# Late value tiles spread over 21 units of the score pass, and table and weight copies moved off ScalarE

## The chip, the cores and the metric

The kernel runs on one NeuronCore of a Trainium2 chip. Its engines work side by side and are ordered by semaphores alone: TensorE (PE in the profile; PEld is its weight load), VectorE (DVE), ScalarE (ACT), GpSimd (POOL), and SyncE (SP), which issues most transfers. The metric is the device time of one execution in microseconds; where several runs are shown, their median.

## The reference

One transformer block on x of 4 x 1024 tokens with 256 features, in float32. Cut to what matters:

```python
x = x + _layernorm(attention(_layernorm(x)))          # 16 heads of 16 dims, rotary positions
    q, k, v = x @ Wq.T + bq, x @ Wk.T + bk, x @ Wv.T + bv     # q and k then rotated
    attn = softmax(q @ k.T / 4); out = (attn @ v) @ Wo.T + bo
x = x + _layernorm(moe(_layernorm(x)))                # 8 experts of hidden size 684
    dist = sqrt(squared distance of each token to 8 centroids)
    w, sel = top_k(dist, 2); w = softmax(w)           # the two farthest centroids
    out = sum over the two: w * ((silu(x @ Wg + bg) * (x @ W1 + b1)) @ W2 + b2)
```

## The kernel before, in words

**Start.** The 4096 tokens are cut into 8 blocks (NB) of 512. For each, VectorE takes the statistics (`stats`, L881 and L884), ScalarE the standard deviation (`deviation`, L1274), VectorE its inverse and the offset (`invert`, L888 and L890), and ScalarE writes the normalised rows (`normalise`, L1281). TensorE turns them (`turn_x`, L1482), ScalarE copies them out of PSUM (`save_xt`, L1287), and TensorE projects q and k (`project`, L1493), which VectorE rotates (`rope_unit`, L912 to L921) with GpSimd (L724, L729) and ScalarE (`high`, L1301). Three things must be ready once: the cosine and sine tables, turned by TensorE into four PSUM banks (L1469) and copied to SBUF (L1316); the q and k weights and biases in rotation order (L1307, L1311); and the biases as columns, by four small matmuls into bank 6 (L1474), copied by L1318. ScalarE does all eleven of these copies, between `deviation(0)` and `normalise(0)`.

**Value tiles.** `project_v(m, half)` (L1509) projects 256 tokens to the values of all heads: four matmuls of 128x256 (eight records in the trace), saved by ScalarE (`save_v`, L1294), stored by SP (`store_v`, L465). The first four tiles (EARLY_V = 2 blocks) are made within the start; the other twelve are late.

**Score pass.** The scores are made twice. The first pass finds the row maxima: `max_scores` (L1528) writes, for unit m and pair a, two matmuls of 48x512 into two banks, and VectorE reduces the pair with one instruction (`reduce_max`, L942). There are two pairs of banks (4 and 5, 6 and 7), and

```python
if half == 0:
    after(pe, s_max, 2 * (UNITS * g + m) + a - 1)
```

lets TensorE refill a pair only when the reduce of the unit before has read it. A group (four heads of one batch element) has UNITS = 16 units. The main loop makes the scores of group g again, with exponentials and weighted sums (L1540, L1346, L1554), and in the same units the first pass of what lies LEAD = 5 units ahead of the next group. So before the main loop stand 16 units of group 0 and 5 of group 1: 21 units. The twelve late value tiles stand there too, one behind each of units 0 to 11. TensorE waits for all late tiles to be saved before the main loop. The maxima, split and turned (L753, L755, L948), go through DRAM into the stacks (`load_max_rows`, L492 and L497), once for each half of a group.

Every engine has its own instruction list, in the order in which the code of its block is written: nothing is reordered by a scheduler.

## Time and profile before

| | us |
|---|---|
| median of three runs | 1600.58 (1593.86 to 1622.9) |
| the profiled execution, whole | 1592.43 |
| its span, first to last instruction | 1590.5 |
| mean granted TensorE clock over the span | 0.949 |

The span falls into the start (to about 98 us), the first score pass (to 155), the main loop over 16 groups (to about 800), the output projection with norms and routing (to about 955) and the experts. All times below are from the span's start. The granted clock is a share of 2.4 GHz: 1.00 is the upper of its two levels, 0.50 the lower (1.2 GHz).

### The profile page before, as it was taken

The page shows a single profiled execution, that of the slowest core. Times are in us where ns is not written, and L with a number is a line of the kernel's source. Part 1 is how long each engine was busy: PE and PEld are TensorE (multiplying, and loading weights), DVE is VectorE, ACT ScalarE, POOL GpSimd, SP SyncE. Part 2 cuts the span into 40 slices and gives each one's busy share as a digit, 9 for nine tenths or more (in the row PEclk, how much of TensorE's full clock was granted, in tenths as well). Part 3 has the DMA queues.
Part 4 walks back from the last instruction along what each step waited for, and adds up shares of the span by engine and source line. Part 5 has one row for each costly group of instructions (what it writes and reads, how often), then busy time and mean ns, then how long its engine had stood idle before and what let it go on. Part 6 is the DMA issues. An engine that isn't in the chain of part 4 may idle for free.

```text
span 1590.5 us, 29998 instructions
## 1 busy us (share of the span) xinstructions
PE 1446.7 (91%) x9435; PEld 800.9 (50%) x9436; DVE 1107.6 (70%) x1978; ACT 852.3 (54%) x1624; POOL 427.4 (27%) x411
## 2 busy tenths in 40 slices
PE   7989999999999999999999438999999999999950
PEld 4444333333333333333355226777777777777740
DVE  5989899999999989999026774555555555455525
ACT  5531788888888878888865321222222222222215
POOL 3760000000000010001014143444444444444425
PEclk9997899999999999999999759999999999999985
DMA  5887146334545554550429623222212222121136
GB/s 171 241 254 129 44 98 169 65 71 81 88 82 89 100 88 64 82 89 16 158 54 213 225 98 91 33 33 33 31 32 33 33 33 33 33 33 31 32 85 199
DMA packets 125116, 141.80 MB, mean 89 GB/s; under 512 B 55131, under 2 KB 98949, under 8 KB 125030
## 3 DMA queue, kind: packets, MB, share of 16 engines
q1 hardware_dynamic: 109126, 121.98, 33.2%
q0 software_dynamic: 15904, 18.66, 7.2%
q8 instruction: 56, 0.92, 0.2%
q14 instruction: 30, 0.25, 0.1%
HBM read 86.30 MB, written 54.30 MB: 88 GB/s over the span
## 4 chain that ended last, share of the span: by engine, by line
PE 78%; DVE 7%; issue 5%; ACT 4%; DMA 2%; SPq 2%; POOL 1%; DVEq 0%; POOLq 0%; ACTq 0%
PE psum L1681 20%; PE psum L1528 18%; PE psum L1554 16%; PE psum L1700 11%; PE psum L1691 3%; PE psum L1509 2%; PE psum L1540 2%; PE psum L1612 1%; PE psum L1493 1%; ACT work L1346 1%; DVE mx L942 1%; ACT weights L1356 1%; PE psum L1667 1%; PE psum L1610 1%; DVE work L1141 1%
## 5 line engine op out<-in xcount | busy, mean ns | idle before, releaser
L942 DVE TENSOR_REDUCE mx<-psum 128x1 f32<-128x1024 f32 x512 | 622.9, 1222 | 29.2 <-PE psum L1528 26.3
L1346 ACT ACTIVATE work<-psum 128x512 f32<-128x512 f32 x1024 | 556.7, 597 | 106.1 <-PE psum L1540 43.8
L1528 PE MATMUL psum<-stack 48*128 48x512 f32 x1024 | 379.3, 457 | 6.7 <-DVE mx L942 6.0
L1540 PE MATMUL psum<-stack 50*128 50x512 f32 x1024 | 379.1, 450 | 0.0
L1681 PE MATMUL psum<-weights,values 128*128 x1136 | 341.1, 454 | 0.6 <-DVE values L1161 0.6
L1554 PE MATMUL psum<-work,values 128*32 128x256 f32 x4096 | 330.5, 395 | 9.2 <-ACT weights L1356 9.2
L1528 PEld LDWEIGHTS psum<-stack 48*128 48x128 f32 x1024 | 154.2, 191 | 221.7 <-DVE mx L942 184.7
L1681 PEld LDWEIGHTS psum<-weights,values 128*128 128x128 f32 x1136 | 211.8, 192 | 99.2 <-issue 3.1
L1423 ACT ACTIVATE values<-values 128x342 f32<-128x342 f32 x142 | 69.3, 488 | 250.1 <-DVE values L1173 250.1
L1700 PE MATMUL psum<-weights,work 114*128 (+1 forms) x852 | 198.7, 383 | 1.3 <-ACT work L1434 0.8
L1554 PEld LDWEIGHTS psum<-work,values 128*32 128x32 f32 x4096 | 82.5, 108 | 198.2 <-ACT work L1346 100.5
L1700 PEld LDWEIGHTS psum<-weights,work 114*128 114x128 f32 (+1 forms) x852 | 158.0, 192 | 21.3 <-issue 1.8
L1540 PEld LDWEIGHTS psum<-stack 50*128 50x128 f32 x1024 | 153.8, 188 | 17.3 <-ACT work L1346 17.3
L829 POOL DMA_INDIRECT values<-xn_d,at_x x71 | 70.0, 986 | 280.9 <-DVE at_w L1204 275.5
L1429 ACT ACTIVATE work<-psum,dots 128x256 f32<-128x256 f32 x71 | 33.6, 473 | 201.3 <-PE psum L1700 196.7
L1173 DVE TENSOR_TENSOR values<-psum,work 128x342 f32<-128x342 f32 x142 | 73.1, 515 | 92.0 <-PE psum L1681 68.1
L836 POOL DMA_INDIRECT y_d<-work,at_y x71 | 115.2, 1622 | 39.7 <-issue 27.2
L1176 DVE TENSOR_TENSOR values<-psum,work 128x342 f32<-128x342 f32 x142 | 73.1, 515 | 62.2 <-PE psum L1681 62.2
L1192 DVE COPY work<-psum 114x256 f32<-114x256 f32 x71 | 30.2, 425 | 118.2 <-PE psum L1691 118.2
L753 POOL CAST m<-mx 128x16 fp32r<-128x16 f32 x32 | 6.3, 197 | 376.4 <-DVE mx L942 376.4
L1181 DVE TENSOR_TENSOR values<-values 128x342 f32<-128x342 f32 x142 | 73.3, 516 | 14.7
L744 POOL TENSOR_TENSOR values<-weights,dots 128x512 f32<-128x512 f32 x16 | 20.5, 1283 | 225.4 <-issue 225.2
(184 smaller groups left out, 1190.6 us busy)
## 6 DMA issues: line engine op xcount, KB each, us to landing
stack<-qk_scr SPq DMA_DIRECT2D x192, 128.0 KB, 6.1
qk_scr<-weights SPq DMA_DIRECT2D x16, 1024.0 KB, 4.8
weights<-in_w SPq DMA_DIRECT2D x8, 1368.0 KB, 7.1
ot_scr<-weights SPq DMA_DIRECT2D x16, 512.0 KB, 3.2
weights<-in_w SPq DMA_DIRECT2D x8, 684.0 KB
work<-in_b SPq DMA_DIRECT2D x8, 684.0 KB, 8.8
y_d<-zeros SPq DMA_DIRECT2D x1, 4224.0 KB, 14.3
v_scr<-weights SPq DMA_DIRECT2D x32, 128.0 KB, 2.5
```

The costliest lines, as they stand in the source:

```text
L829: pool.indirect_dma_start(out=x_row, out_offset=None, in_=xn2_d, in_offset=bass.IndirectOffsetOnAxis(ap=at_x[:, 0:1], axis=0)).then_inc(s_ ...
L836: pool.indirect_dma_start(out=y_d, out_offset=bass.IndirectOffsetOnAxis(ap=at_y[:, 0:1], axis=0), in_=y_row, in_offset=None, compute_op=AL ...
L942: dve.tensor_reduce(mx[:, r, a, t:t + 1], bank(4 + 2 * a, 2), AX, ALU.max, negate=True).then_inc(s_max, 1)
L1173: dve.tensor_tensor(gates[c], bank(2 * c)[:, 0:CH], bias(0), ALU.add).then_inc(s_gb, 1)
L1176: dve.tensor_tensor(hid[:, CH * c:CH * (c + 1)], bank(2 * c + 1)[:, 0:CH], bias(HID), ALU.add).then_inc(s_ub, 1)
L1181: dve.tensor_tensor(hid[:, CH * c:CH * (c + 1)], hid[:, CH * c:CH * (c + 1)], gates[c], ALU.mult).then_inc(s_hid, 1)
L1346: act.activation(pt[u % 4][:, j, :], bank((c + HG * u + n) % 3), ACT.Exp, scale=SC).then_inc(s_exp, 1)
L1528: ins = pe.matmul(bank(4 + 2 * a + half), qs[t3][at:at + QROWS, r, P * t:P * (t + 1)], ks[t3][at:at + QROWS, r, 512 * half:512 * (half + 1 ...
L1540: pe.matmul(bank((t3 + HG * u + n) % 3), ks[t3][at:at + MROWS, r, P * st:P * (st + 1)], qs[t3][at:at + MROWS, r, 512 * half:512 * (half + ...
L1554: last = pe.matmul(bank(3)[32 * j:32 * (j + 1), at:at + 256], vg[p][:, st, j, :], pt[u % 4][:, j, at:at + 256], start=st + part == 0, stop ...
L1681: last = pe.matmul(dst, x_t[:, k, :], w1_sb[:, bass.ds(e, 1), k, col:col + CH].rearrange("p a n -> p (a n)"), start=k == 0, stop=k == KC - 1)
L1700: last = pe.matmul(bank(7)[:, 0:C], h_t[0:rows, k, :], w2_sb[0:rows, bass.ds(e, 1), k, :].rearrange("p a n -> p (a n)"), start=k == 0, sto ...
```

## The change

Three edits. The eleven copies leave ScalarE: GpSimd reorders the weights and the bias row (six copies), VectorE copies the four tables and the bias columns, right behind `invert(0)`; TensorE makes the bias columns behind `turn_x(0)` instead of ahead of it. The twelve late value tiles are spread over all 21 units by an integer rule: behind units 1, 3, 5, 6, 8, 10, 12, 13, 15, 17, 19 and 20. And SP sends the two maxima loads of group 0 behind the stores of blocks 3 and 5 instead of 5 and 7.

```diff
@@ -584,9 +584,8 @@
             load_stacks(sp, 0, 1)
             for m in range(EARLY_V, NB):
                 store_v(sp, m)
-                if m == 5:
-                    load_max_rows(sp, 0, 0, 0)
-            load_max_rows(sp, 0, 0, 1)
+                if m in (3, 5):
+                    load_max_rows(sp, 0, 0, (m - 3) // 2)
             sp.wait_ge(s_ones, 3)
             load_stacks(sp, 0, 2)
             for parts_of in s_pst:
@@ -714,6 +713,15 @@
                 pool.wait_ge(s_pad, n + 1)
             pool.memset(cent_t[:, :, :], 0.0).then_inc(s_pad, 1)
 
+            pool.wait_ge(s_wqkv, 32)
+            for k in range(KC):
+                for i in range(2):
+                    pool.tensor_copy(w_turn[:, k, i, :, :].rearrange("p s (d h) -> p s d h", h=H),
+                                     w_qkv[:, k, C * i:C * (i + 1)].rearrange("p (h s d) -> p s d h", s=2, d=HALF)).then_inc(s_wp, 1)
+            for i in range(2):
+                pool.tensor_copy(b_turn[0:1, i, :, :].rearrange("p s (d h) -> p s d h", h=H),
+                                 b_row[0:1, C * i:C * (i + 1)].rearrange("p (h s d) -> p s d h", s=2, d=HALF)).then_inc(s_wp, 1)
+
             def rotate(w):
 
                 p = w % 2
@@ -923,6 +931,11 @@
             stats(0)
             spread_tables()
             invert(0)
+            for n, (table, at) in enumerate(((cos_t, 0), (cos_t, 512), (sin_t, 0), (sin_t, 512))):
+                dve.wait_ge(s_tab, n + 1)
+                dve.tensor_copy(table[:, at:at + 512], bank(n)).then_inc(s_tabs, 1)
+            dve.wait_ge(s_bt, 1)
+            dve.tensor_copy(b_c[:, :], bank(6)[:, 0:4]).then_inc(s_bc, 1)
             stats(1)
             invert(1)
             for m in range(NB):
@@ -1301,21 +1314,6 @@
                 act.activation(hl[w % 4][:, 0, :, :].bitcast(F32R), rr[w % 2], ACT.Copy).then_inc(s_hi, 1)
 
             deviation(0)
-            act.wait_ge(s_wqkv, 32)
-            for k in range(KC):
-                for i in range(2):
-                    act.activation(w_turn[:, k, i, :, :].rearrange("p s (d h) -> p s d h", h=H),
-                                   w_qkv[:, k, C * i:C * (i + 1)].rearrange("p (h s d) -> p s d h", s=2, d=HALF),
-                                   ACT.Copy).then_inc(s_wp, 1)
-            for i in range(2):
-                act.activation(b_turn[0:1, i, :, :].rearrange("p s (d h) -> p s d h", h=H),
-                               b_row[0:1, C * i:C * (i + 1)].rearrange("p (h s d) -> p s d h", s=2, d=HALF),
-                               ACT.Copy).then_inc(s_wp, 1)
-            for n, (table, at) in enumerate(((cos_t, 0), (cos_t, 512), (sin_t, 0), (sin_t, 512))):
-                act.wait_ge(s_tab, n + 1)
-                act.activation(table[:, at:at + 512], bank(n), ACT.Copy).then_inc(s_tabs, 1)
-            act.wait_ge(s_bt, 1)
-            act.activation(b_c[:, :], bank(6)[:, 0:4], ACT.Copy).then_inc(s_bc, 1)
             normalise(0)
             save_xt(0)
             deviation(1)
@@ -1468,12 +1466,6 @@
                     src = spread[n // 2][:, 4 * (n % 2) + a, :, :].rearrange("p d h -> p (d h)")
                     last = pe.transpose(bank(n)[:, P * a:P * (a + 1)], src, ident[:, :])
                 last.then_inc(s_tab, 1)
-            pe.wait_ge(s_wp, 6)
-            for i in range(2):
-                for s in range(2):
-                    last = pe.matmul(bank(6)[:, 2 * i + s:2 * i + s + 1], b_turn[0:1, i, s, :], ones_f[0:1, 0:1], start=True, stop=True)
-            last.then_inc(s_bt, 1)
-
             def turn_x(m):
                 pe.wait_ge(s_xn, TB * (m + 1))
                 for k in range(KC):
@@ -1511,6 +1503,12 @@
                 last.then_inc(s_vp, 1)
 
             turn_x(0)
+            pe.wait_ge(s_wp, 6)
+            for i in range(2):
+                for s in range(2):
+                    last = pe.matmul(bank(6)[:, 2 * i + s:2 * i + s + 1], b_turn[0:1, i, s, :], ones_f[0:1, 0:1], start=True, stop=True)
+            last.then_inc(s_bt, 1)
+
             for m in range(NB):
                 project(2 * m)
                 if m + 1 < NB:
@@ -1582,12 +1580,13 @@
                 for m in range([UNITS, LEAD][g]):
                     for n in range(HG):
                         max_scores(g, g, m, n // 2, n % 2)
-                    b = 2 * EARLY_V + m
-                    if g == 0 and b < 2 * NB:
-                        if m == 0:
-                            pe.wait_ge(s_r1, NU)
-                            pe.wait_ge(s_x1, NU)
-                        project_v(b // 2, b % 2)
+                    unit = UNITS * g + m
+                    late = 2 * (NB - EARLY_V)
+                    if unit == 0:
+                        pe.wait_ge(s_r1, NU)
+                        pe.wait_ge(s_x1, NU)
+                    for b in range(late * unit // (UNITS + LEAD), late * (unit + 1) // (UNITS + LEAD)):
+                        project_v(EARLY_V + b // 2, b % 2)
             pe.wait_ge(s_va, 2 * NB)
             pe.wait_ge(s_pad, 2)
             groups(pe, group)
```

The start on TensorE, before the change (L1469 turns the tables, L1474 makes the bias columns, L1482 turns x, L1493 projects):

```order
L1469 MATMUL psum<-ident,work 128x128 [waits tables_spread]
L1469 MATMUL psum<-ident,work 128x128 x7
L1474 MATMUL psum<-ones_f,work 128x1 [waits weights_ordered]
L1474 MATMUL psum<-ones_f,work 128x1 x3
L1482 MATMUL psum<-ident,work 128x128 [waits xn_ready]
L1482 MATMUL psum<-ident,work 128x128 x7
L1493 MATMUL psum<-weights,work 128x512 [waits tables_saved,xn_t_ready]
```

The same place in the change (L1467, L1509, L1474 and L1485 are its lines for the same four):

```order
L1467 MATMUL psum<-ident,work 128x128 [waits tables_spread]
L1467 MATMUL psum<-ident,work 128x128 x7
L1474 MATMUL psum<-ident,work 128x128 [waits xn_ready]
L1474 MATMUL psum<-ident,work 128x128 x7
L1509 MATMUL psum<-ones_f,work 128x1 [waits weights_ordered]
L1509 MATMUL psum<-ones_f,work 128x1 x3
L1485 MATMUL psum<-weights,work 128x512 [waits tables_saved,xn_t_ready]
```

The turning of x no longer stands behind the reordered weights; the bias columns now stand between it and the first projection.

VectorE at the start of the change (L936 copies the tables, L938 the bias columns; the statistics of the second block, L889, followed L898 directly before):

```order
L896 RECIPROCAL work<-work 128x4 [waits std_ready]
L898 SCALAR_TENSOR_TENSOR work<-work 128x4 [waits rstd_ready]
L936 COPY work<-psum 128x512 [waits tables_turned] x4
L938 COPY b_c<-psum 128x4 [waits bias_columns]
L889 BN_STATS work<-weights 128x6 [waits x_loaded1]
```

What moved in is two waits on TensorE, for the turned tables and for the bias columns, ahead of the second block's statistics.

The score pass on TensorE, units 0 to 3 before the change (L1528 is a pair of score matmuls, L1509 a value tile):

```order
L1528 MATMUL psum<-stack 128x512 x3
L1509 MATMUL psum<-work,weights 128x256 [waits v_saved,second_by_cosine,second_rotated]
L1509 MATMUL psum<-work,weights 128x256 x3
L1528 MATMUL psum<-stack 128x512 [waits max_done]
L1528 MATMUL psum<-stack 128x512
L1528 MATMUL psum<-stack 128x512 [waits max_done]
L1528 MATMUL psum<-stack 128x512
L1509 MATMUL psum<-work,weights 128x256 [waits v_saved]
L1509 MATMUL psum<-work,weights 128x256 x3
```

The same units in the change (L1526 is the pair, L1501 the tile):

```order
L1526 MATMUL psum<-stack 128x512 x3
L1526 MATMUL psum<-stack 128x512 [waits max_done,second_by_cosine,second_rotated]
L1526 MATMUL psum<-stack 128x512
L1526 MATMUL psum<-stack 128x512 [waits max_done]
L1526 MATMUL psum<-stack 128x512
L1501 MATMUL psum<-work,weights 128x256 [waits v_saved]
L1501 MATMUL psum<-work,weights 128x256 x3
L1526 MATMUL psum<-stack 128x512 [waits max_done]
L1526 MATMUL psum<-stack 128x512
L1526 MATMUL psum<-stack 128x512 [waits max_done]
L1526 MATMUL psum<-stack 128x512
L1526 MATMUL psum<-stack 128x512 [waits max_done]
```

Behind every pair of pairs stood a tile; now two units' pairs stand between most tiles.

## Rows read from the trace of the kernel before

**Rows 1.** The page, part 1: busy us, share of the span, instructions.

```profile
PE 1446.7 (91%) x9435; PEld 800.9 (50%) x9436; DVE 1107.6 (70%) x1978; ACT 852.3 (54%) x1624; POOL 427.4 (27%) x411
```

**Rows 2.** Timeline of ScalarE, the start: start us, us, engine, line, operation, count, [idle before].

```profile
8.11 0.30 ACT L1274 ACTIVATE work<-work,eps 128x4 f32<-128x4 f32 x1
9.12 2.23 ACT L1307 ACTIVATE work<-work 128x256 f32<-128x256 f32 x4 [0.72 <-DMA work<-in_bqkv]
...
14.42 2.06 ACT L1281 ACTIVATE work<-weights,work 128x256 f32<-128x256 f32 x4
```

**Rows 3.** Timeline of TensorE, the start.

```profile
7.45 3.65 PE L1469 MATMUL psum<-ident,work 128*128 128x128 f32 x16 [7.45 <-DVE work L897]
12.45 1.86 PE L1474 MATMUL psum<-ones_f,work 1*128 1x1 f32 x8 [1.35 <-ACT work L1311]
16.53 1.97 PE L1482 MATMUL psum<-ident,work 128*128 128x128 f32 x8 [2.22 <-ACT work L1281]
19.18 5.61 PE L1493 MATMUL psum<-weights,work 128*128 128x512 f32 x8 [0.69 <-ACT weights L1287]
```

**Rows 4.** Timeline of VectorE, the start.

```profile
8.64 0.16 DVE L890 SCALAR_TENSOR_TENSOR work<-work 128x4 f32<-128x4 f32 x1
10.55 1.41 DVE L881 BATCH_NORM_STATS2 work<-weights 128x6 f32<-128x256 f32 x4 [1.74 <-DMA weights<-in_x]
...
23.12 0.75 DVE L912 SCALAR_TENSOR_TENSOR work<-psum,b_c,work 128x512 f32<-128x512 f32 x1 [1.80 <-PE psum L1493]
```

**Rows 5.** Timeline of GpSimd, the start.

```profile
0.81 0.31 POOL L696 MEMSET zeros<- 128x256 f32 x1 [0.29 <-POOLq L1760]
...
25.75 1.27 POOL L724 TENSOR_TENSOR work<-work 128x512 f32<-128x512 f32 x1 [20.43 <-DVE work L915]
```

**Rows 6.** Timeline of TensorE, the first score pass.

```profile
94.29 0.73 PE L1528 MATMUL psum<-stack 48*128 48x512 f32 x4
98.50 3.50 PE L1509 MATMUL psum<-work,weights 128*128 128x256 f32 x8 [3.48 <-DVE work L921]
101.93 0.73 PE L1528 MATMUL psum<-stack 48*128 48x512 f32 x4
102.59 1.99 PE L1509 MATMUL psum<-work,weights 128*128 128x256 f32 x8
104.52 1.32 PE L1528 MATMUL psum<-stack 48*128 48x512 f32 x4
...
131.51 2.00 PE L1509 MATMUL psum<-work,weights 128*128 128x256 f32 x8
...
136.61 0.73 PE L1528 MATMUL psum<-stack 48*128 48x512 f32 x2 [0.40 <-DVE mx L942]
...
138.87 3.56 PE L1528 MATMUL psum<-stack 48*128 48x512 f32 x6 [0.40 <-DVE mx L942]
```

**Rows 7.** Timeline of VectorE: the pass's first unit, and the main loop.

```profile
98.36 2.35 DVE L942 TENSOR_REDUCE mx<-psum 128x1 f32<-128x1024 f32 x2
...
174.11 13.53 DVE L942 TENSOR_REDUCE mx<-psum 128x1 f32<-128x1024 f32 x11 [0.42 <-PE psum L1528]
```

**Rows 8.** Timeline of ScalarE: the save of the last value tile, and behind it.

```profile
133.54 0.60 ACT L1294 ACTIVATE weights<-psum 128x512 f32<-128x512 f32 x1 [2.09 <-PE psum L1509]
134.16 1.28 ACT L1346 ACT_TABLE_LOAD   x1
```

**Rows 9.** Windows: stretch, length, busy us of each engine, granted clock, DMA share, GB/s.

```profile
150.00:155.00 5.00, 4.80 (x9) 1.99 (x8) 4.83 (x5) 0.00 (x0) 0.00 (x0) 0.50 1.04 146
...
575.00:600.00 25.00, 24.46 (x208) 8.82 (x208) 21.81 (x20) 18.85 (x35) 0.42 (x2) 0.86 0.61 88
```

**Rows 10.** Timeline of TensorE: first instruction of the main loop, and of its sixth unit.

```profile
155.36 0.76 PE L1528 MATMUL psum<-stack 48*128 48x512 f32 x1 [0.18 <-DVE mx L942]
...
173.34 0.49 PE L1528 MATMUL psum<-stack 48*128 48x512 f32 x1
```

**Rows 11.** Timeline of SP's queue: the second maxima rows of group 0 sent.

```profile
145.22 0.34 SPq L492 DMA_DIRECT2D m_scr<-m_t  x1
```

## Prediction

> **What bounds the kernel now.** I read the page first: TensorE is busy for 1446.7 of the 1590.5 us [rows 1]. Busy time doesn't say what a moved instruction is worth, so I then read the timelines of the two stretches that the change touches.
>
> The first is the start. ScalarE takes the square root for the first norm at 8.11 us, but normalises x only at 14.42: from 9.12 on it reorders weights and copies tables [rows 2]. TensorE waits meanwhile: the tables are turned by 11.10, the bias columns (L1474) end at 14.31, the turning of x starts at 16.53, the first projection at 19.18 [rows 3], and VectorE begins its first rotation at 23.12 [rows 4]. This stretch is a chain through ScalarE.
>
> The second is the first score pass: 16 units of group 0 and 5 of group 1, before the main loop. In each unit VectorE reduces two pairs of banks, and TensorE refills a pair only when it has been reduced. After units 0 to 11 TensorE also projects one late value tile. A tile goes from 102.59 to the next pair at 104.52, so it takes 1.93 us, and from 102.59 to 131.51 there are ten such units, 2.89 us each [rows 6]; VectorE needs 2.35 for its two reduces [rows 7], so TensorE sets the pace. In the nine units without a tile VectorE sets it, 2.26 per unit (136.61 to 138.87). But from 139 us a pair takes 1.19 (3.56 for three) instead of 0.66 (101.93 to 102.59) [rows 6]: the granted clock is down to 0.50, the lower of the two levels, after a stretch of short bursts with waits between, and it has not come back at 150 to 155 [rows 9]. The main loop starts at 155.36 with it; its first five units take until 173.34 [rows 10].
>
> **The start, term one: -4.0 us.** ScalarE loses its eleven copies, so the norm can follow VectorE's offset, ready at 8.80 [rows 4]: 8.85 + 2.06 [rows 2] = 10.9. TensorE is free of the tables at 11.10, turns x in 1.97 (13.1), then does the bias columns, now behind it, in 1.86 (14.9), and projects there instead of at 19.18 [rows 3]: 4.2 us earlier. What must be there by then:
> - GpSimd's six copies, from the landing of the weights at 9.1. No row shows such a copy: 128x256 costs 0.31 as a fill, and at most as much as the two-input 128x512 at 1.27 [rows 5]. Six make 1.9 to 7.6 us, ready at 11.0 to 16.7. I take half of the two-input row, 0.64 each, since it is one input of half the size: ready at 13.0, in time. At the far end the projection comes at 18.6 and the gain is 0.6.
> - VectorE's four table copies: PSUM operands of 128x512 cost it 0.75 [rows 4], and the last follows the turning at 11.1, so about 11.9. Then it waits for the bias columns with the second block's statistics queued behind (they ran at 10.55 before, with nothing waiting). Copy, statistics, inverse and the third block's statistics are 0.2 + 1.8 + 0.7 + 1.8 by the same kinds of rows, so its first rotation starts near 19.4, 3.7 earlier than 23.12. The second block's norm is then ready at 16.9 + 0.3 + 0.4 + 2.06 = 19.7, and the first projection ends by 14.9 + 5.61 = 20.5: 0.8 to spare, so that is late next.
>
> I take 4.0. Everything up to the score pass shifts with it; the stack of group 0 was loaded long before its use at 94.29 [rows 6], which follows the projection without a wait.
>
> **The score pass at the upper clock, term two: +3.7 us.** The twelve tiles now stand behind units 1, 3, 5, 6, 8, 10, 12, 13, 15, 17, 19 and 20. A tile isn't hidden behind the reduces, for two pairs is all that PSUM holds: with a bare unit between, the chain is second pair 0.66, tile 1.93, next pair until its data are out 0.77 (0.73 and a hand-over, 0.03 where the last tile at 133.51 meets its save at 133.54 [rows 8]), two reduces 2.35, hand-over 0.05: 5.76 us for a tile unit and a bare one [rows 6, 7]. Before, the two cost 2.89 + 2.26 = 5.15: neighbouring tiles overlap better, since after one of them both pairs are free at once. Count: unit 0 2.3; eight runs with the bare unit behind 46.1; two second tiles 2.6 each; the last two units 3.5 and 2.6. That is 59.7 from the first reduce. TensorE then waits for the save of the last tile, 0.60 on ScalarE [rows 8] with two hand-overs, less its overlap 1.0 in all: the loop would start at 98.36 [rows 7] + 59.7 + 1.0 = 159.1, against 155.36. (ScalarE's table load, 1.28, hid in its idle time [rows 8]; now it follows the last save beside the first scores, 0.5 late and recovered by units that wait for VectorE.) With term one the loop starts at 155.1: the two cancel. The bounds: all tiles hidden, 21 units at 2.26 or 47.5, is -8.5 for this term; every tile costing its full 1.93 beside them is +15.
>
> **The clock in the loop, term three: -2.9 us.** Five units take 17.98 us, nearly all at the lower clock [rows 10], and at the later pace of 2.46 a unit (eleven reduces in 13.53, two to a unit [rows 7]) 12.3. The whole 5.7 comes back if the clock is up at the loop's start. Tiles in units 19 and 20 favour that, but the wait for the save and two units without weighted sums follow. I take half.
>
> **The clock in the pass, term four: +8 us.** Between tiles TensorE now runs three bursts of 0.66 in 3.84 us. That is much like 136.61 to 139, a burst every 1.13, after which the clock fell. It also fell for some microseconds after a single pause of the main loop (0.86 in 575 to 600 [rows 9]). A tile brings it back: after the idle stretch before 98.50 the first one took 3.50, the next 1.93 [rows 6]. At the lower level a run costs 1.19 + 3.50 + 1.30 + 2.35 + 0.05 = 8.39, or 2.6 more. I take three falls at that price. The bounds are none (0) and all nine runs with three second tiles, some +30. The Trainium skill, TensorE: Matmul & The Clock Gate, section "A second HAM failure mode: psum-queue depth-cycling", tells of a kernel whose matmul groups cycle through PSUM with small idles and whose clock goes back and forth between the two levels: it speaks against this spreading. By that rule the clock would go down and up with the tiles, some 1597; without it this term is nothing and the sum is 1589. The trace agrees as far as the fall at 139 goes.
>
> **The rest: 0.** SP's order changes: the group's second maxima rows go out before the last two value stores. They were sent at 145.22 [rows 11], ten us ahead of the loop, and keep five units of cover; if that is gone, the first scores wait some us. The third stack is sent after the last tile, a few us behind the loop's start, but is needed eleven units (27 us) later.
>
> **Sum:** -4.0 + 3.7 - 2.9 + 8 = +4.8. The profiled execution's 1592.4 becomes 1597.2. The runs shown stand 1.4 to 30 above that execution, their median 8.2; I forecast **1598 us**, no change.
>
> **Rivals.**
> - *The clock holds (0.22).* No fall in the pass and none in the loop: -4.0 + 3.7 - 5.7, 1586.4. For it: a tile in more than every second unit, nowhere two bare units in a row. Against: the fall at 139.
> - *The tiles hide (0.08).* VectorE paces all 21 units: start of the loop at 98.4 - 4.0 + 47.5 + 1.0 = 142.9, 12.5 earlier, and 5.7 in the loop: 1574.2. For it: over all 21 units TensorE's work is the smaller, 21 x 0.66 + 12 x 1.93 = 37 us. Against: the chain of 5.76, which needs a third pair of banks to break.
> - *The clock stays down (0.15).* It falls at the first gap and the tiles are too far apart to bring it back, as pairs alone did not from 139 to 155. -4.0 + 3.7 + 30 with nothing won in the loop: 1622, slower than before. It is decided by whether one tile lifts the clock; half the pass at the lower level is enough for 1607.
> - *The start does not move (0.07).* GpSimd's copies take the far end, or VectorE's wait for the bias delays the second block as much as the first gains: 1592.4 + 8.8 = 1601.
>
> **How the numbers follow.** The forecast holds 0.48. The range of 1585 to 1614 leaves out the hidden tiles and the upper half of the clock that stays down, and takes in the spread of the runs. A measurement of this kernel can tell some 2% (32 us) from no change. No case gains that much: faster 0.02. Only the clock that stays down, with a run like the higher ones shown, comes near it on the other side: slower 0.03. The same: 0.95.
>
> **What would show it.** In the new profile: the first projection near 15 us and the first rotation near 19.4; GpSimd's copies at 0.3 to 0.7; tile units of 3.5 and bare ones of 2.3 where the clock is up, VectorE idle about 1.2 us per tile; the clock at 0.50 in some stretches of the pass; the loop's start between 155 and 170. Wrong would be: reduces back to back through the tiles (they hide), 0.50 throughout (the clock stays down), or a first projection after 18.

## The result, and the profile after

The changed kernel is slower: median 1636.05 us (1621.71 to 1677.91, four runs) against 1599.49 (four runs of the kernel before), a ratio of 1.0205 with the interval 1.0137 to 1.0273. Measured again beside another set of runs of the kernel before, it took 1619.15 (1614.12 to 1622.36), ratio 1.0117 (1.0044 to 1.0191). The ratios leave out executions more than 1.5% above the fastest of their kernel, the medians do not. Both intervals lie above 1; whether the loss is over 2% is open. The profiled execution took 1621.71 us with a span of 1619.9, which is 29.5 over the span before; its mean granted clock is 0.933 against 0.949. The two traces account for the 29.5:

| | before, us | after, us | change of the stretch that ends here |
|---|---|---|---|
| first reduce of the score pass | 98.36 | 92.29 | -6.1 |
| main loop starts | 155.36 | 170.74 | +21.4 (pass 57.00, then 78.45) |
| unit 8 of the loop | 180.72 | 197.34 | +1.2 |
| group 10 starts | 562.03 | 578.59 | 0 |
| group 11 starts | 606.96 | 627.95 | +4.4 |
| group 14 starts | 727.28 | 748.25 | 0 |
| group 15 starts | 768.93 | 799.86 | +10.0 |
| end of the span | 1590.47 | 1619.93 | -1.5 |

Part 1 of the page after [rows 1]: TensorE is busy 20 us longer with the same 9435 instructions.

```profile
PE 1467.1 (91%) x9435; PEld 807.0 (50%) x9436; DVE 1111.5 (69%) x1983; ACT 847.4 (52%) x1613; POOL 431.4 (27%) x417
```

**The start** came out better than forecast. Timelines of the changed kernel, ScalarE [rows 2]:

```profile
8.97 2.08 ACT L1294 ACTIVATE work<-weights,work 128x256 f32<-128x256 f32 x4 [0.44 <-DVE work L898]
```

TensorE [rows 3]:

```profile
11.11 1.23 PE L1474 MATMUL psum<-ident,work 128*128 128x128 f32 x8
12.82 1.05 PE L1509 MATMUL psum<-ones_f,work 1*128 1x1 f32 x8 [0.48 <-POOL work L722]
13.79 3.70 PE L1485 MATMUL psum<-weights,work 128*128 128x512 f32 x8
18.56 1.09 PE L1474 MATMUL psum<-ident,work 128*128 128x128 f32 x8 [1.06 <-ACT work L1294]
```

VectorE [rows 4]:

```profile
11.27 0.69 DVE L936 COPY work<-psum 128x512 f32<-128x512 f32 x1 [0.16 <-PE psum L1467]
13.90 0.16 DVE L938 COPY b_c<-psum 128x4 f32<-128x4 f32 x1 [1.94 <-PE psum L1509]
...
18.64 0.72 DVE L920 SCALAR_TENSOR_TENSOR work<-psum,b_c,work 128x512 f32<-128x512 f32 x1
```

GpSimd [rows 5]:

```profile
9.34 2.30 POOL L719 COPY work<-work 128x256 f32<-128x256 f32 x4 [4.01 <-DMA work<-in_bqkv]
11.59 1.17 POOL L722 COPY work<-work 1x256 f32<-1x256 f32 x2
```

The norm starts at 8.97 instead of 14.42, GpSimd's copies take 0.58 each, and the first projection stands at 13.79 instead of 19.18. It also takes 3.70 instead of 5.61, because the clock now goes up at 11.4 us instead of 23.1. The next block is turned at 18.56 (before, at 24.64): these 6.1 us are the gain at the first reduce, though TensorE waits 1.06 there for the block's norm.

**The pass** is where the time went. TensorE [rows 6]:

```profile
111.55 3.78 PE L1501 MATMUL psum<-work,weights 128*128 128x256 f32 x8
115.26 1.23 PE L1526 MATMUL psum<-stack 48*128 48x512 f32 x4
116.41 2.38 PE L1501 MATMUL psum<-work,weights 128*128 128x256 f32 x8
...
122.56 1.99 PE L1501 MATMUL psum<-work,weights 128*128 128x256 f32 x8
124.48 0.74 PE L1526 MATMUL psum<-stack 48*128 48x512 f32 x4
126.53 0.73 PE L1526 MATMUL psum<-stack 48*128 48x512 f32 x2 [1.31 <-DVE mx L955]
127.66 1.22 PE L1526 MATMUL psum<-stack 48*128 48x512 f32 x2 [0.40 <-DVE mx L955]
128.81 3.78 PE L1501 MATMUL psum<-work,weights 128*128 128x256 f32 x8
```

VectorE [rows 7]; the number in brackets is its idle time before the instruction:

```profile
116.51 2.36 DVE L955 TENSOR_REDUCE mx<-psum 128x1 f32<-128x1024 f32 x2 [3.63 <-PE psum L1526]
119.48 3.49 DVE L955 TENSOR_REDUCE mx<-psum 128x1 f32<-128x1024 f32 x3 [0.61 <-PE psum L1526]
...
125.25 3.49 DVE L955 TENSOR_REDUCE mx<-psum 128x1 f32<-128x1024 f32 x3 [1.06 <-PE psum L1526]
128.92 1.23 DVE L955 TENSOR_REDUCE mx<-psum 128x1 f32<-128x1024 f32 x1 [0.18 <-PE psum L1526]
133.78 2.36 DVE L955 TENSOR_REDUCE mx<-psum 128x1 f32<-128x1024 f32 x2 [3.63 <-PE psum L1526]
```

The pass before, as a window (length, then busy us of TensorE, its weight loads, VectorE, ScalarE and GpSimd, granted clock, DMA share, GB/s):

```profile
98.36:155.36 57.00, 53.87 (x177) 31.11 (x178) 48.93 (x45) 10.34 (x15) 13.31 (x12) 0.83 0.74 158
```

Windows of the changed kernel [rows 9]: the whole pass, two pieces of it, the loop's first units, and groups 10 and 14.

```profile
92.30:170.74 78.44, 63.78 (x176) 37.73 (x177) 49.27 (x45) 9.32 (x15) 13.28 (x12) 0.72 0.42 95
...
117.20:127.50 10.30, 7.25 (x30) 4.18 (x28) 8.63 (x9) 1.20 (x2) 0.42 (x2) 1.00 0.38 83
127.50:141.20 13.70, 12.23 (x28) 7.20 (x30) 7.18 (x7) 0.65 (x2) 0.00 (x0) 0.50 0.18 39
...
175.30:192.40 17.10, 17.10 (x96) 5.45 (x94) 10.38 (x10) 9.31 (x18) 0.42 (x2) 0.50 0.61 94
...
591.70:608.80 17.10, 17.10 (x96) 5.46 (x96) 10.42 (x9) 8.69 (x16) 0.00 (x0) 0.50 0.85 120
...
762.40:786.30 23.90, 23.90 (x136) 7.70 (x132) 14.19 (x12) 13.04 (x25) 0.00 (x0) 0.50 0.01 1
```

From 117.2 to 127.5 the clock is at its upper level and a tile takes 1.99; a reduce behind a tile starts at 119.48, the next at 125.25, 5.77 for a tile unit and a bare one (forecast 5.76). Then the clock falls, a tile takes 3.78 and VectorE waits 3.63 for it. In the trace's record of the clock there are seven falls in the pass, at 93.4, 103.6, 110.4, 127.5, 148.0, 154.8 and 161.6 us, of 44.4 us together. VectorE's work in the pass is what it was (49.27 us; 48.93 before); its idle time grew from 8.1 to 29.2.

### The profile page after: what moved, and what is told of

It is laid out like the page before. It is cut to its first block, busy times and chain, and to the rows that moved or that the text cites. A ratio compares the mean times of both kernels' runs of the same rounds, so it can differ in the third digit from the quotient of the medians.

```text
span 1619.9 us, 29998 instructions
## 1 busy us (share of the span) xinstructions
PE 1467.1 (91%) x9435; PEld 807.0 (50%) x9436; DVE 1111.5 (69%) x1983; ACT 847.4 (52%) x1613; POOL 431.4 (27%) x417
## 4 chain that ended last, share of the span: by engine, by line
PE 79%; DVE 7%; issue 5%; ACT 3%; DMA 2%; POOL 2%; SPq 1%; DVEq 0%; POOLq 0%; ACTq 0%
PE psum L1680 20%; PE psum L1526 18%; PE psum L1552 16%; PE psum L1699 11%; PE psum L1690 3%; PE psum L1501 3%; PE psum L1538 2%; PE psum L1611 2%; DVE mx L955 1%; ACT work L1344 1%; PE psum L1485 1%; ACT weights L1354 1%; PE psum L1666 1%; PE psum L1609 1%; DVE work L1154 1%
## 5 line engine op out<-in xcount | busy, mean ns | idle before, releaser
L1526 PE MATMUL psum<-stack 48*128 48x512 f32 x1024 | 382.7, 464 | 21.5 <-DVE mx L955 20.8
L1538 PE MATMUL psum<-stack 50*128 50x512 f32 x1024 | 386.4, 457 | 0.7 <-ACT work L1344 0.7
L1552 PE MATMUL psum<-work,values 128*32 128x256 f32 x4096 | 338.3, 404 | 8.9 <-ACT weights L1354 8.9
L1526 PEld LDWEIGHTS psum<-stack 48*128 48x128 f32 x1024 | 155.7, 195 | 240.2 <-DVE mx L955 181.9
L761 POOL CAST m<-mx 128x16 fp32r<-128x16 f32 x32 | 6.4, 199 | 413.2 <-DVE mx L955 413.2
L752 POOL TENSOR_TENSOR values<-weights,dots 128x512 f32<-128x512 f32 x16 | 20.5, 1285 | 225.3 <-issue 225.1
## 6 DMA issues: line engine op xcount, KB each, us to landing
y_d<-zeros SPq DMA_DIRECT2D x1, 4224.0 KB, 14.4
```

The lines of the kernel that those rows point to most:

```text
L1526: ins = pe.matmul(bank(4 + 2 * a + half), qs[t3][at:at + QROWS, r, P * t:P * (t + 1)], ks[t3][at:at + QROWS, r, 512 * half:512 * (half + 1 ...
L1538: pe.matmul(bank((t3 + HG * u + n) % 3), ks[t3][at:at + MROWS, r, P * st:P * (st + 1)], qs[t3][at:at + MROWS, r, 512 * half:512 * (half + ...
L1552: last = pe.matmul(bank(3)[32 * j:32 * (j + 1), at:at + 256], vg[p][:, st, j, :], pt[u % 4][:, j, at:at + 256], start=st + part == 0, stop ...
```

## The experiments

The theory: the pass is longer because a lone tile stands between two refills, with only two pairs of banks, and, for the larger part, because the clock falls in the units between tiles. Each figure below of a stretch is from the one profiled execution of a kernel, to be held against 1592.43 us of the profile before; the other executions can lie some way off, as the medians show. Each ratio is to runs of the kernel before that were taken beside it.

| kernel | profile, us | median, us | ratio to before (interval) | pass, us | loop starts |
|---|---|---|---|---|---|
| start edit alone | 1586.89 | 1588.57 | 0.9987 (0.9934 to 1.004) | 57.45 | 149.67 |
| spread alone | 1612.80 | 1617.83 | 1.0101 (1.0046 to 1.0156) | 78.29 | 175.87 |
| change, clock held up | 1590.64 | 1595.63 | 0.9975 (0.9926 to 1.0024) | 62.16 | 154.06 |
| change, tiles in pieces | 1644.10 | 1636.44 | 1.0201 (1.0088 to 1.0314) | 98.23 | 190.85 |
| change again | 1622.36 | 1619.15 | 1.0117 (1.0044 to 1.0191) | 78.74 | 171.06 |
| change, third pair | 1607.18 | 1589.41 | 0.9961 (0.9916 to 1.0006) | 55.96 | 149.73 |
| before, filled bare units | 1594.76 | 1602.39 | 1.0000 (0.9956 to 1.0044) | 58.36 | 157.03 |
| change, loop delayed | 1605.19 | 1617.00 | 1.0095 (1.0050 to 1.0141) | 81.62 | 174.16 |
| change, divisions moved | 1600.78 | 1602.51 | 1.0029 (0.9996 to 1.0062) | 78.34 | 170.19 |
| start, divisions moved | 1578.95 | 1590.36 | 0.9911 (0.9853 to 0.9968) | 58.49 | 150.83 |
| change, third pair, divisions moved | 1575.87 | 1579.71 | 0.9875 (0.9771 to 0.9978) | 54.41 | 147.15 |
| start, filled units, divisions moved | 1571.80 | 1589.14 | 0.9921 (0.9870 to 0.9973) | 57.09 | 149.69 |

**One part alone.** The start edit without the spread is the change with these two pieces put back:

```diff
-                    for b in range(late * unit // (UNITS + LEAD), late * (unit + 1) // (UNITS + LEAD)):
-                        project_v(EARLY_V + b // 2, b % 2)
+                    b = 2 * EARLY_V + m
+                    if g == 0 and b < 2 * NB:
...
+                        project_v(b // 2, b % 2)
...
-                if m in (3, 5):
-                    load_max_rows(sp, 0, 0, (m - 3) // 2)
+                if m == 5:
+                    load_max_rows(sp, 0, 0, 0)
+            load_max_rows(sp, 0, 0, 1)
```

> The kernel before with the start edit alone (weight order on GpSimd, table copies on VectorE, bias columns after the first transposes); the value tiles run in the first ten units as before. Theory 1, the spread tiles cost the time: the first reduction stands near 92.3 us as after the change, the first score pass takes the 57 us of the kernel before, the main loop starts near 149, and the execution is about 6 us shorter than the kernel before, a ratio near 0.996. Rival, the start edit costs the pass its time (an earlier start against transfers that land no earlier): the pass takes over 65 us and the loop starts at 157 or later. For the clock falls at groups 10 and 14: if they belong to the spread pass they are as short here as before (6.8 us and none); if they belong to the shift in time or to chance, at least one is over 15 us.

The spread without the start edit is the kernel before with the same two pieces the other way round.

> The kernel before with the spread of the value tiles and the earlier second row of maxima alone; the start is that of the kernel before. Theory 1, the spread tiles cost the time: first reduction at 98.4, the pass takes 75 to 81 us in place of 57, the main loop starts near 175, the execution is at least 20 us longer than the kernel before, a ratio of 1.013 or more. Rival, the start edit is needed for the loss: the pass takes under 65 us and the ratio stays under 1.005.

The stretches came as theory 1 had them; of the spread's ratio, forecast at 1.013 or more, 1.0101 was measured. The start edit alone has its first reduce at 92.21 and keeps the pass of before, 57.45; every later stage is 5.7 us early, and the clock's falls in the loop are those of before. Over the executions its ratio cannot be told from 1. The spread alone has its first reduce at 97.58 and a pass of 78.29. So the spread, with SP's new order, makes the loss of the pass, and the start edit has no share in that. The loss at groups 10 and 14 is another matter: they took 44.92 and 41.68 us with the start edit alone, 44.95 and 41.67 with the spread alone, and 44.93 and 41.65 before, so in the traces those 14.4 us came only with both edits together. SP's order was not undone by itself; the group's second maxima are sent at 153.18 to 154.62 and the loop's first scores wait for ScalarE's last save, so nothing in the trace points to it.

**The clock held up.** The units without a tile get work for TensorE; a `fill` is one matmul of 128x256 into the bank that the next tile overwrites, and its result is never read:

```diff
                     for n in range(HG):
                         max_scores(g, g, m, n // 2, n % 2)
+                    done = 2 * (NB - EARLY_V) * (UNITS * g + m) // (UNITS + LEAD)
+                    if UNITS * g + m > 0 and done == 2 * (NB - EARLY_V) * (UNITS * g + m + 1) // (UNITS + LEAD):
+                        for _ in range(2):
+                            fill(2 * EARLY_V + done)
```

> The changed kernel with two extra matmuls of 128x256 (results never read, written to the bank that the next value tile overwrites) in every unit of the first score pass that has no value tile, so that TensorE's work per unit is more even. Theory 1a, the loss is the granted clock that falls in the units without a tile: the clock stays at the upper level through the pass, the tiles take 1.93 us and not 3.5 to 3.8, the pass takes about 61 us, the main loop starts near 153, about 18 us sooner than in the changed kernel; the execution is 1597 to 1605. Rival 1b, an isolated tile stands in the chain from reduction to refill whatever the clock: VectorE still waits 2.8 to 3.6 us at each tile and the pass takes over 72 us. Rival 1c, half each: 65 to 70 us.

Windows of this kernel, the pass and the part of it behind the one fall:

```profile
91.89:154.06 62.17, 55.83 (x210) 33.53 (x210) 48.99 (x45) 9.33 (x15) 13.32 (x12) 0.95 0.53 120
...
99.60:154.06 54.46, 49.48 (x198) 29.57 (x196) 44.29 (x40) 6.87 (x13) 7.94 (x9) 1.00 0.50 98
```

More work on TensorE made the pass 16.3 us shorter. The granted clock is 1.00 from 99.60 on, VectorE's idle time is 13.2 in place of 29.2, and the pass is 62.2 against a forecast of 61. The profile, 1590.64, came out under its range of 1597 to 1605: groups 10 and 14 cost what they cost before. Rivals 1b and 1c fall: of the 21.4 us that the pass lost, some 16 are the clock and some 5 the lone tile, with whatever the extra matmuls cost.

**A third pair of banks** (banks 2 and 3, free once the rotations end; tiles in banks 0 and 1; `at_k` counts the pairs, `lead` is true in the first pass; not shown: reduces and saves read the new banks, and the wait for the last rotations stands ahead of the first pair):

```diff
-                    after(pe, s_max, 2 * (UNITS * g + m) + a - 1)
-                ins = pe.matmul(bank(4 + 2 * a + half), qs[t3][at:at + QROWS, r, P * t:P * (t + 1)],
+                    after(pe, s_max, at_k - 2 if lead else 2 * (UNITS * g + m) + a - 1)
+                ins = pe.matmul(bank(2 + 2 * (at_k % 3) + half if lead else 4 + 2 * a + half), qs[t3][at:at + QROWS, r, P * t:P * (t + 1)],
...
-                    dst = bank((b - 2 * EARLY_V) % 4)
+                    dst = bank(b % 2)
```

> The changed kernel with a third pair of banks for the scores of the first pass (banks 2 and 3 beside 4 to 7) and the value tiles in banks 0 and 1 in turn. Theory 1, two pairs leave no room for a tile between two refills: with a third, VectorE has a filled pair waiting while a tile runs, TensorE's work comes closer together and its clock stays at the upper level; the pass takes 50 to 56 us, main loop at 142 to 148, the execution 1578 to 1587. Rival, the clock falls all the same in the units without a tile, and a tile of 3.7 us at the lower level is longer than the 2.4 us of reductions that a third pair holds: the pass takes 60 to 70 us, loop start 153 to 162. Rival, the value tiles with two banks wait for their saves on ScalarE: TensorE idle before the tiles, ended by ScalarE, over 0.5 us each.

The pass took 55.96 us with VectorE idle for 7.2, in the range of theory 1:

```profile
93.77:149.73 55.96, 48.64 (x178) 29.80 (x176) 48.74 (x44) 8.81 (x15) 12.82 (x11) 0.88 0.58 127
```

The clock did not stay up throughout, as theory 1 had it: it fell four times for 3.4 us. The loop's start missed its range by 2 us, since the first refill now waited for the last rotation (first reduce at 93.77). The profiled execution, the slowest of ten, missed it by 20 (their median by 2): against the kernel before the loop lost 6.8 us up to unit 12, to a fall of 30.7 us, and 13.2 at groups 10 and 14.

**The tiles in pieces**; a `piece` is one matmul of a tile, 128x256:

```diff
+                        at = 2 * (UNITS * g + m) + n // 2 - 1
+                        if n % 2 == 1 and 0 <= at < slots:
...
+                            for q in late[len(late) * at // slots:len(late) * (at + 1) // slots]:
+                                piece(*q)
-                    for b in range(late * unit // (UNITS + LEAD), late * (unit + 1) // (UNITS + LEAD)):
-                        project_v(EARLY_V + b // 2, b % 2)
```

> The changed kernel with each value tile cut into its matmuls of 128x256, one or two of them after each pair of score blocks of the first pass, in place of a tile of four in a row at the end of a unit. Theory 1, the tile as a lump of 1.9 to 3.8 us between two refills is what VectorE waits for: single matmuls of about 0.5 us fit into TensorE's idle time beside a reduction, VectorE runs its 40 reductions back to back (40 times 1.18 is 47 us), the pass takes 48 to 53 us, the main loop starts at 141 to 146, and the execution is 1570 to 1585, a ratio near 0.985. Rival, the values' saves on ScalarE or the bank that a tile needs set the pace: the pass stays over 60 us even at the upper clock. Rival, the small pieces do not hold the clock up: granted clock 0.50 in half of the pass or more, refills of 1.9 us each, the pass takes 65 us or more.

The theory failed here, and the last rival won: the pass took 98.23 us. Windows, and TensorE's timeline with its weight loads:

```profile
100.00:180.00 80.00, 80.00 (x145) 37.34 (x144) 38.99 (x35) 5.97 (x10) 8.25 (x9) 0.50 0.35 68
```

```profile
120.14 0.50 PEld L1526 LDWEIGHTS psum<-stack 48*128 48x128 f32 x2 [0.65 <-issue]
120.14 1.22 PE L1526 MATMUL psum<-stack 48*128 48x512 f32 x2
121.29 1.35 PEld L1583 LDWEIGHTS psum<-work,weights 128*128 128x128 f32 x4 [0.65 <-issue]
121.29 2.07 PE L1583 MATMUL psum<-work,weights 128*128 128x256 f32 x4
```

The clock fell at 94.8 and stayed at 0.50 for 116 us, although the profile shows TensorE busy without a break from 100 to 180. The same tiles in one run of four matmuls each, two such units in a row, were followed by its rise in the changed kernel (111.55 to 118.79, up at 117.2). Why the pieces do not lift it is not shown.

**The bare units of the kernel before filled:**

```diff
                         max_scores(g, g, m, n // 2, n % 2)
+                        if UNITS * g + m >= 2 * (NB - EARLY_V) and n % 2 == 1:
+                            fill(2 * NB)
```

> The kernel before (value tiles in the first ten or twelve units in a row) with one extra matmul of 128x256, result never read, after each pair of score blocks in the units without a tile. Theory, in the kernel before these bare units are what lets the clock fall (at 139.1 us for 34.1 us), and the loop's first units pay for it with 18.0 us for three units from unit 2 to the end of unit 5 and the five before, while at the upper clock they take about 12.3: with the extra matmuls the clock stays at the upper level, the pass stays at 57 to 59 us, and the loop is ahead by 4 to 7 us from unit 5 on. Rival, the extra matmuls delay the refills as much as the clock gives back: the loop's unit 5 within 2 us of the kernel before. Rival, the clock falls at the loop's start whatever stands before it (the first units wait for ScalarE's table load): a fall of 10 us or more between 155 and 175.

The clock stayed up (0.97 over the pass of 58.36), but from the loop's start to unit 5 only 3.5 us came back, 1.84 net, so the forecast of 4 to 7 failed and the first rival (within 2 us) held. A fall of 6.8 us at 160.9 remained.

**The later falls.** The changed kernel was profiled once more, unchanged.

> The changed kernel once more, unchanged. Question: are the 4.4 us at group 10 and the 9.9 us at group 14 of its first profile its own or chance of that execution? If chance of where the clock's falls land: the pass again takes about 78 us and the loop starts near 171, but the falls at groups 10 and 14 are 6.8 us and none as in the kernel before, and the execution is near 1607 in its profile. If they belong to the change: both come again, 17 and 24 us long within 4 us, and no execution is under 1618.

Every fall came again within 0.4 us of its place, 17.1 us long at 592.0 and 23.9 at 762.7. So this is no accident of one execution. (That no execution is under 1618 did not hold: two of four took 1614 and 1616, so the falls of those two were not all the same.) Next the loop was moved in time:

```diff
             pe.wait_ge(s_pad, 2)
+            for _ in range(7):
+                pe.matmul(bank(0)[:, 0:C], xn_t[:, 2, 0, 0:P], w_qkv[:, 0, 2 * C:3 * C], start=True, stop=True)
             groups(pe, group)
```

> The changed kernel with seven extra matmuls of 128x256 (results never read) between the first pass and the main loop, to move all of the loop by 1.7 to 3.5 us without changing it. If the length of the clock falls at groups 10 and 14 hangs on where in time the same stalls land, the two falls differ from the 17.1 and 23.9 us of the changed kernel by 7 us or more, and the loop's constant offset from group 1 to 10 is 18 to 20 us over the kernel before. If the falls belong to the change's loop itself they stay at 17 and 24 us.

And last, the stall ahead of the falls was taken away:

```diff
                         split_max(g + 1, r)
+                        if r == 0 and g in (10, 14):
+                            norm_o((g - 10) // 4)
...
-                if g in (9, 13):
-                    norm_o((g - 9) // 4)
```

> The changed kernel with GpSimd's two division steps (2.4 us each, after the value copies of groups 9 and 13, ahead of the next group's split of the maxima) moved between the two splits of the group behind, where GpSimd waits some 16 us. Theory: groups 10 and 14 stall because that split comes late, and the clock falls in the wake of that stall; without the stall both groups take the 40.1 us of the others, so the changed kernel loses 9.3 us at group 10 and 11.5 us at group 14, 20.8 together, and its profile stands near 1600 us; the first pass stays at 78 us. Rival: the clock falls of the changed kernel there are not tied to this stall: groups 10 and 14 keep over 44 us, the profile stays over 1612.

The stall on GpSimd in the changed kernel: its divisions (L782) hold up the split of the maxima (L761) to 589.69,

```profile
585.02 4.74 POOL L782 TENSOR_TENSOR weights<-weights 128x1024 f32<-128x1024 f32 x2
589.69 0.21 POOL L761 CAST m<-mx 128x16 fp32r<-128x16 f32 x1
```

and VectorE, which may not overwrite the maxima before, waits 1.91 us and starts the next reduces at 590.37, then waits 0.94 before each of the next seven:

```profile
590.24 0.21 DVE L961 STREAM_TRANSPOSE m_t<-m 128x32 f32<-128x32 f32 x1 [1.91 <-POOL m L763]
590.37 3.67 DVE L955 TENSOR_REDUCE mx<-psum 128x1 f32<-128x1024 f32 x3
594.98 1.23 DVE L955 TENSOR_REDUCE mx<-psum 128x1 f32<-128x1024 f32 x1 [0.94 <-PE psum L1526]
```

VectorE in the changed kernel with the loop delayed, behind the same stall:

```profile
587.78 16.76 DVE L955 TENSOR_REDUCE mx<-psum 128x1 f32<-128x1024 f32 x14
```

GpSimd with the divisions moved, where the split no longer waits for them:

```profile
586.79 0.20 POOL L761 CAST m<-mx 128x16 fp32r<-128x16 f32 x1 [2.23 <-DVE mx L955]
...
587.25 4.72 POOL L782 TENSOR_TENSOR weights<-weights 128x1024 f32<-128x1024 f32 x2
```

The delay cost 3.4 us at the loop's start and the loop was still faster: its first eight units took 20.55 us (26.60 in the changed kernel), so group 10 started 2.6 us earlier than there and not later, 14.0 over the kernel before where 18 to 20 had been forecast. Fourteen reduces ran back to back behind the stall, the fall at group 10 was gone and that at group 14 was 6.8 us. Groups 10 and 14 took 41.96 and 44.60 us in place of 49.36 and 51.61. So the same stall can be followed by falls of very different length. At group 10 the traces show 6.8 us before and with the start alone, the spread alone or the clock held up, 13.7 with the bare units filled, 17.1 twice in the change, 20.5 with the third pair, and none here. Two of these kernels, the clock held up and the bare units filled, started group 10 within 0.12 us of each other (560.07 and 560.19) and had 6.8 and 13.7, so the time since the start does not settle the length by itself; what does stays open. (Of the ten executions of the delayed kernel six took 1616.7 to 1618.1, so the falls may come back in most; only one was traced.) With the stall gone the two groups took 40.40 and 40.08, 20.5 us less than in the changed kernel, and nine of ten executions took 1600.2 to 1603.9. The theory holds: the divisions' stall, there before too, is what let the clock fall at these groups. The change does not make the stall; that it only shifted when the stall came fits all the traces, but is not shown by itself.

**Better versions.** The moved divisions with the start edit alone,

> The start edit alone, with the same move of GpSimd's division steps. The start gives 5.7 us as measured in the start edit alone, the two stalled groups give 4.8 and 1.5 us more where the theory of the late split holds: profile at 1579 to 1582, about 12 us under the kernel before, and a ratio of 0.990 to 0.994. Rival: the division steps where they now stand delay another step (the second split, the next value copies): some group from 11 on takes over 42 us, and the profile is over 1584.

with the change on three pairs, now in an order (banks 6, 4, 6, then 2, 4, 6 in turn) in which the first refill waits for no rotation (cut, against the first try),

```diff
+                base = 6 if at_k == 0 else 2 + 2 * (at_k % 3) if lead else 4 + 2 * a
-                ins = pe.matmul(bank(2 + 2 * (at_k % 3) + half if lead else 4 + 2 * a + half), qs[t3][at:at + QROWS, r, P * t:P * (t + 1)],
+                ins = pe.matmul(bank(base + half), qs[t3][at:at + QROWS, r, P * t:P * (t + 1)],
```

> The changed kernel with the third pair of banks in another order (the pair in banks 2 and 3 comes third, so that the first refill waits for no rotation of the last block), and the division steps moved. Against the first try with three pairs: first reduction at 92.3 and not 93.8, the pass 54 to 57 us, main loop at 146 to 149, groups 10 and 14 without a stall; the loop's first units may still run at the lower clock (6 us). Profile 1574 to 1584. Rival: the first pass gives nothing back since its end is set by the last saves of values: loop start at 149 or later, profile 1584 or more.

and with the start edit and the filled bare units, each piece as shown above:

> The start edit, value tiles in a row as in the kernel before, one extra matmul (result never read) after each pair of score blocks in the units without a tile, and the division steps moved. If the gains add (start 5.7, loop's first units 1.8 net, the two stalls 6.3): 13 to 14 us under the kernel before, profile 1577 to 1580, ratio 0.989 to 0.993. Rival: the extra matmuls give nothing on top of the start edit and the moved divisions: within 1 us of that kernel.

All three beat both kernels; their intervals overlap, so the order among them is open. The first two profiles came as expected (1578.95 just under its range), with medians some 4 to 11 us above them. VectorE with three pairs reduces through a tile:

```profile
114.47 10.36 DVE L957 TENSOR_REDUCE mx<-psum 128x1 f32<-128x1024 f32 x9
126.47 2.36 DVE L957 TENSOR_REDUCE mx<-psum 128x1 f32<-128x1024 f32 x2 [1.65 <-PE psum L1531]
```

The third profile did better than its 13 to 14 us: 20.6. But it was the fastest of ten executions, and their median of 1589.14 is that of the start edit with the divisions moved (1590.36): over the executions no gain of the extra matmuls shows. Its window over the pass has the clock at the upper level throughout, and it stayed there to 880 us; from the loop's start to unit 5 it took 11.7 us, and 18.0 before.

```profile
92.60:149.69 57.09, 56.95 (x213) 34.08 (x213) 49.77 (x45) 10.35 (x15) 13.32 (x12) 1.00 0.75 159
```

## Why the prediction was wrong, by its steps

- **Term one, -4.0: right, undersized.** Measured -6.1 at the first reduce. GpSimd's copies were 0.58 (taken as 0.64); the rest is work that I priced by rows at the lower clock: turning x 1.23 (1.97), bias columns 1.05 (1.86), the first projection 3.70 (5.61). The second block's norm, named as late next with 0.8 to spare, was late: TensorE waited 1.06 us for it.
- **Term two, +3.7: right in its chain.** The 5.76 were measured as 5.77; with the clock held up, but with extra matmuls and one early fall of 6.8 us, the pass was 5.2 longer than before, so the 3.7 by itself is not shown. That "two pairs is all that PSUM holds" was wrong: a third pair fitted in banks 2 and 3 and broke the chain (55.96 and 54.41).
- **Term four, +8: this step failed.** The price of a run at the lower clock was about right (8.39 forecast; 8.53 from the reduces at 125.25 to those at 133.78), the number was not: I took three falls, because one tile had brought the clock back at 98.50 [rows 6]. That tile had eleven others behind it, one in every unit. A lone tile brought it back only sometimes: after the one at 128.81 it stayed down to 141.2. The pass had 44.4 us at the lower level, 57% of it, and that cost about 16, some six runs' price in place of three. The sentence on the rival that the clock stays down, that half the pass at the lower level gives 1607, was nearest to what came, and the rival had a chance of only 0.15: without the losses at groups 10 and 14 the profile after is 1621.7 - 14.4 = 1607.3. That the profile's 1621.7 is also the 1622 of that rival is luck, since the rival has the clock down all through the pass and nothing at groups 10 and 14. The rule of the Trainium skill, TensorE: Matmul & The Clock Gate, "A second HAM failure mode: psum-queue depth-cycling", held: the windows go back and forth between 1.00 and 0.50. I had turned it into three falls; here it was seven.
- **Term three, -2.9: wrong sign.** The loop's first eight units lost 1.2. The clock was up at 168.4 to 175.3, then fell for 17.1 us. That the 5.7 was there to be had is shown by the traced execution of the last kernel, where the first five units took 11.7 in place of 18.0.
- **Not in the sum: the stalls at groups 10 and 14, +14.4.** I read the window at 575 to 600 at 0.86 [rows 9] only as a sign that a pause lets the clock fall, and took the loop behind unit 5 as a constant. It isn't: at group 10 the stall with its fall cost 4.8 us before and 9.3 after.
- **The rest, 0:** no cost was seen.
- **From the sum to the forecast.** The 1597.2 is a sum for the profiled execution, but a median was forecast, and the median shown stood 8.2 above that execution. The 1598 carries 0.8 of this; after the change the two medians stood 14.3 above the execution profiled with them and 3.2 under it.

## What to carry to other kernels

Before spreading a block of dense matmuls through a stage that waits for another engine, price the stage at both clock levels and count the stretches without dense work: here, with extra matmuls in both and the clock up for nearly all of it, the spread pass took 62.16 us and the block in a row 57.09, and the lower clock cost the spread some 16 more. If it must be spread, give the stage a spare buffer first (a third pair made the same spread 22 us shorter). And look for stalls far behind an edit: one that costs 2 us by itself cost 9 to 12 with its clock fall, and moving two steps of 2.4 us to where their engine waits took it away in the traced execution of each of the four kernels that had the move.

## What the runs showed of the hardware

- A TensorE that the profile shows as busy for 80.00 of 80 us, with single matmuls of 128x256 between pairs of 48x512, was granted 0.50 all through; adding work in other places (the filled units) brought 1.00 over 54 us. Busy time in the profile is no sign of the clock.
- The clock's falls can repeat exactly: two traced executions of one kernel, on different occasions, had the same thirteen falls within 0.4 us. They need not: other executions of that kernel took 1614 to 1638 us at mean clocks of 0.938 to 0.920. With the loop delayed, so that group 10 started 2.6 us and group 14 ten us earlier, one fall went from 17.1 us to none and another from 23.9 to 6.8.
